# Attention turns: the score maxima from four packed groups of 32 rows, one bank per head, instead of sixteen full-height tiles

## The reference, cut to what matters

```python
x = x + jnp.tanh(g_xattn[0]) * _L0_xattn_ref(_layernorm(x), ctx_1024, ctx_1024, ...)
x = x + jnp.tanh(g_ffn[0])   * _L0_ffn_ref(_layernorm(x), ...)
x = x + jnp.tanh(g_xattn[1]) * _L1_xattn_ref(_layernorm(x), ctx_1024, ctx_1024, mask, ...)
x = x + jnp.tanh(g_ffn[1])   * _L1_ffn_ref(_layernorm(x), ...)
```

```python
scores = jnp.einsum('bhqd,bhkd->bhqk', q, k) / jnp.sqrt(jnp.float32(D_K))
probs = jax.nn.softmax(scores, axis=-1)
out = jnp.einsum('bhqk,bhkd->bhqd', probs, v)
```

## Time and profile before

| | |
|---|---|
| three runs | 1334.78, 1335.67, 1332.43 us |
| median | 1334.78 us |
| the profiled execution: its span, first to last instruction | 1338.1 us |
| instructions | 28180 |
| mean granted TensorE clock, as a share of full speed | 0.984 |

### The profile page before, as it was taken

One profiled execution on the slowest core, in us unless ns is written; L12 is line 12 of the kernel. 1 busy time (PEld: TensorE's weight loads), 2 busy tenths in 40 slices (PEclk: granted clock), 3 DMA queues, 4 the chain that ended last, 5 costly groups with the idle time before them and its releaser, 6 DMA issues.

```text
span 1338.1 us, 28180 instructions
## 1 busy us (share of the span) xinstructions
PE 1256.4 (94%) x10584; PEld 903.2 (67%) x10584; DVE 886.5 (66%) x1568; ACT 570.1 (43%) x1039; POOL 553.4 (41%) x454
## 2 busy tenths in 40 slices
PE   6999999999999968887999999999997999999997
PEld 6777776777777657621446666766675788888886
DVE  5984677777676455564546766766675977777762
ACT  3255345434442554453553443343336434333331
POOL 3312642553251100000329667955734644454440
PEclk9999999999999998999899999999998999999999
DMA  9865455234411677899983643564414111111100
GB/s 334 231 173 185 140 181 172 74 114 148 140 67 41 206 216 247 297 386 363 400 340 122 220 170 103 163 218 135 126 41 159 63 63 63 63 63 41 53 31 32
DMA packets 126262, 213.58 MB, mean 160 GB/s; under 512 B 27497, under 2 KB 49001, under 8 KB 122091
## 3 DMA queue, kind: packets, MB, share of 16 engines
q1 hardware_dynamic: 126187, 212.57, 47.5%
HBM read 129.92 MB, written 82.62 MB: 159 GB/s over the span
## 4 chain that ended last, share of the span: by engine, by line
PE 81%; DVE 5%; DMA 4%; ACT 4%; issue 3%; SPq 2%; POOL 1%; ACTq 0%; DVEq 0%; POOLq 0%
PE b L157 14%; PE b L158 13%; PE b L159 13%; PE b L1573 5%; PE b L1771 5%; PE b L1772 4%; PE b L1773 4%; PE b L1545 4%; PE b L2067 3%; PE b L1678 3%; PE b L2101 2%; PE b L1686 2%; DMA s_rp<-e_chosen 2%; PE b L2085 2%; PE b L1593 2%
## 5 line engine op out<-in xcount | busy, mean ns | idle before, releaser
L1137 ACT ACTIVATE a_pr<-b 120x512 f32<-120x512 f32 x252 | 130.1, 603 | 95.1 <-PE b L1573 95.1
L1326 DVE TENSOR_REDUCE a_mx<-b 128x4 f32<-128x480 f32 x256 | 151.8, 649 | 12.9 <-PE b L1545 12.8
L1019 POOL TENSOR_TENSOR a_rp<-a_rp,a_b2s 128x512 f32<-128x512 f32 x96 | 120.4, 1293 | 24.9 <-DMA a_rp<-s_rp 24.9
L1058 POOL TENSOR_TENSOR a_atl<-a_pvs,a_ath 128x512 fp32r<-128x512 f32 x64 | 81.2, 1300 | 82.4 <-ACT a_ath L1181 82.4
L1771 PE MATMUL b<-a_woh,a_ath 128*128 128x512 f32 x256 | 104.7, 409 | 3.1 <-POOL a_atl L1058 3.1
L157 PE MATMUL b<-a_xth,a_wqh 128*128 128x512 f32 x256 | 104.0, 406 | 0.3 <-DVE a_xtl L1301 0.3
L1772 PE MATMUL b<-a_wol,a_ath 128*128 128x512 f32 x256 | 101.4, 396 | 0.0
L158 PE MATMUL b<-a_xtl,a_wqh 128*128 128x512 f32 x256 | 101.4, 396 | 0.0
L159 PE MATMUL b<-a_xth,a_wql 128*128 128x512 f32 x256 | 101.4, 396 | 0.0
L1773 PE MATMUL b<-a_woh,a_atl 128*128 128x512 f32 x256 | 101.3, 396 | 0.0
L1003 POOL TENSOR_TENSOR a_rstd<-a_ve,a_mhalf 128x4 f32<-128x4 f32 x16 | 16.2, 1013 | 191.9 <-DVE a_ve L1248 191.9
(11 more groups left out here) (237 smaller groups left out, 3130.5 us busy)
## 6 DMA issues: line engine op xcount, KB each, us to landing
a_rp<-s_rp SPq DMA_DIRECT2D x128, 256.0 KB, 4.5
s_x<-a_x SPq DMA_DIRECT2D x16, 1024.0 KB, 4.3
s_rp<-e_chosen SPq DMA_DIRECT2D x16, 1024.0 KB, 7.9
s_rp<-e_xc SPq DMA_DIRECT2D x16, 1024.0 KB, 7.9
e_w<-in_w SPq DMA_DIRECT2D x56, 256.0 KB, 4.8
a_xr<-in_x_t SPq DMA_DIRECT2D x8, 1024.0 KB, 6.3
a_x<-in_x SPq DMA_DIRECT2D x8, 1024.0 KB, 11.0
s_xn<-a_xn SPq DMA_DIRECT2D x8, 1024.0 KB, 4.8
```

The costliest lines, as they stand in the source:

```text
L1019: pool.tensor_tensor(rp[:, t, a], rp[:, t, a], b2s[:, :], ALU.add).then_inc(rp_biased, 1)
L1058: pool.tensor_tensor(quarter(atl, q), quarter(pvs, q), f(quarter(ath, q)), ALU.subtract).then_inc(a_lo, 1)
L1137: act.activation(pr[:, h % RING, :], bank[k][0:S2, :], ACT.Exp, scale=SCALE)\
L1326: dve.tensor_reduce(mx[:, t, :, r], bank[k][:, 0:HJ * S2].rearrange("p (a s) -> p a s", a=HJ), AX.X, ALU.max).then_inc(free[k], 1)
```

## The change

A new function `max_group` makes the maxima of four heads at once for all 512 queries. Head b of the group uses its own 32 rows of the array and its own bank `s{b}`: the stationary operand is the 32x128 part of `qh`, the moving one the 32x120 block of `kbd`, and query tile t fills columns t*120 to (t+1)*120 of the bank. Sixteen matmuls, t outside and b inside, take the place of four; the last four signal the banks. Before them it waits for the query (`q_hi`) and for all four banks. `maxima` reads the same 480 columns of a bank, which are now four query tiles of one head, and writes them at the transposed place of `mx`.

The order on TensorE is now: query 1, wait for the keys, group 0, query 2, (choices), group 1, query 3, group 2, output tile 0, group 3, output tiles 1 to 3. VectorE alternates the low part of query m with the maxima of group m - 1.

```diff
@@ maxima, VectorE @@
-                dve.tensor_reduce(mx[:, t, :, r], bank[k][:, 0:HJ * S2].rearrange("p (a s) -> p a s", a=HJ),
+                dve.tensor_reduce(mx[:, t, :, r] if i is None else mx[:, :, t, r],
+                                  bank[k][:, 0:HJ * S2].rearrange("p (a s) -> p a s", a=HJ),
                                   AX.X, ALU.max).then_inc(free[k], 1)
@@ turn, VectorE @@
-                queries(j, (1, 2))
-                maxima(i, 0)
-                maxima(i, 1, (0, 1))
-                queries(j, (3,))
-                maxima(i, 1, (2, 3))
-                maxima(i, 2)
+                for m in range(1, C):
+                    queries(j, (m,))
+                    maxima(i, m - 1)
@@ TensorE, new @@
+        def max_group(i, j, r):
+
+            pe.wait_ge(q_hi, C * j + r + 1)
+            for b in range(HJ):
+                k, use = max_bank(i, r, b)
+                pe.wait_ge(free[k], use)
+            for t in range(NT):
+                for b in range(HJ):
+                    k, at = max_bank(i, r, b)[0], slice(b * DK, (b + 1) * DK)
+                    ins = pe.matmul(bank[k][:, t * S2:(t + 1) * S2], qh[at, r, t * P:(t + 1) * P],
+                                    kbd[at, r, b * S2:(b + 1) * S2], start=True, stop=True)
+                    if t == NT - 1:
+                        ins.then_inc(full[k], 1)
@@ turn, TensorE @@
                 queries(i, 1)
+                pe.wait_ge(kbd_in, 16 * HJ * (i + 2))
+                max_group(i, i + 1, 0)
                 queries(i, 2)
             if tail and not last_:
                 choices(i)
             if not last_:
-                pe.wait_ge(kbd_in, 16 * HJ * (i + 2))
-                for t in range(NT):
-                    max_tile(i, i + 1, 0, t)
+                max_group(i, i + 1, 1)
                 queries(i, 3)
-                for t in range(NT):
-                    max_tile(i, i + 1, 1, t)
+                max_group(i, i + 1, 2)
@@ output tiles, behind matmuls m of tile t @@
-                        if t < 2:
-                            max_tile(i, i + 1, 2 + t, m)
+                        if t == 0 and m == C - 1:
+                            max_group(i, i + 1, 3)
```

## The result

The changed kernel took 1355.1 us (median of 4 runs, 1351.5 to 1357.9), the kernel before 1335.2 on the same chip. The ratio is 1.0133, with an interval from 1.0112 to 1.0154: **17.7 us slower**, 15.0 to 20.6 by the interval. The two medians alone lie 19.9 us apart; ratios and intervals stand on record beside the medians and differ from theirs by some 2 us, and this document goes by the ratios. The forecast had the direction, but with +9.4 us it had about half of the size, and its range ended at 1352. The profiled execution of the changed kernel took 1352.4 us, with a span of 1350.6.

What follows compares the result with a forecast made beforehand. TensorE, busy 94% of a 1338.1 us span, was taken as the bound. Terms 6.9 + 0.5 - 0.6 + 2.6 gave +9.4 us on 1334.8, so 1344.2; range 1341 to 1348, or 1337 to 1352 reaching into rivals.

Steps and rivals of the forecast that it cites:

- the wait of a group for VectorE: Before groups in both layers: TensorE waits for VectorE to free the banks, 0.10 to 0.30 us, signal estimated at 0.06.
- the stall for the keys: Ahead of group 0 in layer 1, turns 1 to 5: TensorE idles 0.9 to 1.95 us until the keys land.
- Part 1: TensorE's matmuls in the 14 changed turns: a group costs 0.79 us against four tiles' 0.88, saving 5.7 us in all.
- Part 2: VectorE must free all four banks before each group; waits per turn 0.41 us in layer 0, 0.60 in layer 1.
- -0.1 a turn: Layer 0, turns 1 to 6: waits of 0.41 us against 0.5 saved by the matmuls; -0.6 us in all.
- Part 3: Keys wanted 2.80 us sooner: +6.9 us in layer 1, turns 1 to 5; turn 0 of layer 0 also waits.
- landing is issue plus the time shown: Key loads on SP's queue: landing taken as issue time plus time shown, as 846.4 + 4.2 = 850.6 in turn 3.
- +2.6: Turn 0 of layer 0: the second query falls behind the wait for the keys, so the stretch takes 16.1 us against 13.56.
- Rival 3: Clock falls after layer 1 stalls of 1.4 us and more, four or five times, adding +7 to +8.5 us; chance 0.12.
- Rival 1: VectorE and keys are ahead of TensorE everywhere, so matmuls decide: -5.7 us, 1329.1, or 1298 at quarter price; chance 0.06.

Runs made afterwards that it cites:

- e7: The kernel before, with its old tiles, keys issued amid the experts' loads and the spread's multiplications ahead of query 0's low part; 1340.47 us, ratio 1.0035.
- e1: The kernel before with only TensorE's wait for the next keys moved, from behind query 2 to ahead of it; 1347.93 us, ratio 1.0085.

## Why the prediction was right in direction and short in size

The forecast was +9.4 us, 1344.2, with a range to 1352; measured were 17.7 us by the ratio and a median of 1355.1. The three causes that it named, matmuls, VectorE and keys, are all there. The steps that failed are terms of the sum: the wait of a group for VectorE, where 0.06 us was put behind VectorE's end and 0.14 came; the stall for the keys, where nothing was put between landing and matmul and some 0.4 us came, and where each turn's slack was read from one execution; and the low clock in layer 1, which was left out of the sum as a rival with a chance of 0.12, and came to 3.0 us, 1.5 of them behind a stall for the keys.

**Part 1, TensorE's own work: right.** 0.79 us a group was forecast, and 0.78 measured; 0.34 and 0.5 us a turn were to be saved, and 0.30 and 0.46 are, where nothing waits. The Trainium skill (TensorEngine Tiling (Array Packing), "Theoretical Speedup") gives up to 4x, that is down to a quarter of the tiles' 0.88; the row of the group shows 0.78. The same page ("Key Properties") says that a change of the tiling mode drains the engine, and the edges agree: from 280.59 to the group are 0.32 us where a step is 0.233, and from 281.50 to the next matmul 0.34. A step of 0.33 stands also behind a plain wait without a change of form (278.15 to 278.48 in e7), so the second edge is no more than a restart of the stream takes there.

**Part 2, VectorE: right in kind, mis-sized.** The term "-0.1 a turn" in layer 0 came out as +0.2. TensorE and VectorE there:

```profile
281.66 0.66 PE L1546 MATMUL b<-a_kbd,a_qh 32*128 32x120 f32 x16 [0.31 <-DVE a_pvs L1447]
...
293.11 0.66 PE L1546 MATMUL b<-a_kbd,a_qh 32*128 32x120 f32 x16 [0.21 <-DVE a_mx L1326]
```
```profile
279.04 2.48 DVE L1447 TENSOR_TENSOR a_pvs<-b,a_pvs 128x512 f32<-128x512 f32 x4
...
290.63 2.34 DVE L1326 TENSOR_REDUCE a_mx<-b 128x4 f32<-128x480 f32 x4
```

The multiplications end at 281.52 and the group starts at 281.66; the maxima end at 292.97 and the group starts at 293.11. From VectorE's end to TensorE's start are **0.14 us** both times, and 0.14 to 0.15 ahead of every group that VectorE held in any execution. The forecast had estimated 0.06, between 0.03 and 0.04 of other pairs and 0.08 of a landing. It is no constant of this pair of engines: in e7 VectorE's low part ends at 277.41 + 0.68 = 278.09 and the query tile starts at 278.15, 0.06 later, and the spread of the kernel before, a packed form as well, shows 0.06 in turn 3 of layer 1:

```profile
844.37 1.28 DVE L1432 SCALAR_TENSOR_TENSOR a_rx<-a_rx,a_part,a_rs 128x128 fp32r<-128x128 f32 x1
```
```profile
845.71 0.67 PE L1698 MATMUL b<-a_rx,a_bc 32*128 32x128 f32 x16 [0.26 <-DVE a_rx L1432]
```

In turn 0 of that layer it was 0.15 (709.12 to 709.27). What makes it long ahead of the groups stays open. Against the stretches without a wait, the two waits delay the turn by 0.37 and 0.28 us, where 0.27 and 0.14 were forecast. With the 0.04 less that the matmuls save this is the 0.3 us a turn, 2.0 us in all.

In turns 0 and 6 of layer 1 another step failed too: VectorE's schedule was read in turn 3 and taken for all. VectorE in turn 6, of the kernel before and then of the changed one:

```profile
983.53 0.75 DVE L1316 SCALAR_TENSOR_TENSOR a_ql<-b,a_bq,a_qh 128x512 fp32r<-128x512 f32 x1 [1.70 <-ACT a_qh L1093]
984.20 2.47 DVE L1446 TENSOR_TENSOR a_pvs<-b,a_pvs 128x512 f32<-128x512 f32 x4
```
```profile
996.68 0.75 DVE L1316 SCALAR_TENSOR_TENSOR a_ql<-b,a_bq,a_qh 128x512 fp32r<-128x512 f32 x1 [1.69 <-ACT a_qh L1093]
997.35 2.48 DVE L1447 TENSOR_TENSOR a_pvs<-b,a_pvs 128x512 f32<-128x512 f32 x4
```

Before, the multiplications of this turn end at 984.20 + 2.47 = 986.67, 3.37 us after the query's start at 983.30; in turn 3 it was 3.04, as the low part there was early. So group 0 waits 0.45 us in turn 6 instead of the forecast's 0.10. The answer stood in the trace of before, one turn further on. Together the two turns cost 1.1 us without the clock, 0.6 more than forecast.

**Part 3, the keys: right in kind, the largest term, and short by 2.4 us.** TensorE in the changed kernel, turn 0 of layer 0, then turn 3 of layer 1:

```profile
144.41 0.98 PE L1546 MATMUL b<-a_kbd,a_qh 32*128 32x120 f32 x16 [4.58 <-DMA a_kbd<-s_kh]
...
857.56 0.66 PE L1546 MATMUL b<-a_kbd,a_qh 32*128 32x120 f32 x16 [1.49 <-DMA a_kbd<-s_kh]
```

and the last two key loads of turn 3 on SP's queue, with their time to landing:

```profile
L680 SPq DMA_DIRECT2D a_kbd<-s_kh x2: 316/316/317, 852.4 to 852.8; - x2
DMA to landing us min/median/max: 3.7/4.0/4.3
```

852.8 + 4.3 = 857.1, and the group starts at 857.56. The step that failed is "landing is issue plus the time shown", with nothing behind it: from landing to the matmul are some 0.4 us here, where turn 0 of layer 0 had shown 0.08. Neither the group nor the layer alone makes it: in e1, where a query tile waits for the same keys in layer 1, it is 0.10 to 0.19 us, ahead of the groups there 0.35 to 0.5, and ahead of the groups in turn 0 of layer 0 up to 0.1. The stalls were forecast as 1.95, 1.4, 1.4, 0.9 and 1.4 us, and came as 1.95, 1.26, 1.49, 1.74 and 1.97. Turns 4 and 5 are furthest off, and that is the second half of it: each turn was priced by its own slack in one execution. Before, TensorE waited 0.59 and 0.22 us for the reciprocals ahead of the spread in these turns, which gave the keys time; in the changed kernel it didn't wait there. The way of the keys is nearly the same everywhere: from SP's load of the permutation to group 0 are 857.56 - 838.91 = 18.65 us in turn 3, 18.44 and 18.53 in turns 4 and 5, and 18.66 and 17.96 in turns 1 and 2. The sixteen loads' 11.43 us, the keys and their flight make a chain of nearly fixed length, and this chain, not TensorE, now sets where group 0 starts. Of the 2.4 us, 1.8 are these stalls (8.4 us of idle time for 7.05, and 0.08 more each: idle time counts from the end of the matmul before, 0.40 us behind its start, where a group without a wait comes 0.32 behind it), 0.5 is the wait ahead of group 2 (0.40 us a turn for 0.30) and 0.2 the matmuls' smaller saving.

In turn 0 of layer 0 +1.7 us came for +2.6, since the keys let group 0 start 0.75 us sooner after the spread than the tiles had started in the execution of before. Over six other executions with all the group's columns there, the stretch took 25.01 to 26.62 us, +1.1 to +2.7: this term goes by when the loads land. With tiles it goes by that too: 21.60 us in e7, where the keys were waited for 1.02 us and no clock fell, for 23.95.

**Rival 3, the clock, came in part.** It was priced at four or five falls in layer 1. In turn 4:

```profile
904.95 0.66 PE L1546 MATMUL b<-a_kbd,a_qh 32*128 32x120 f32 x16 [1.74 <-DMA a_kbd<-s_kh]
905.54 0.62 PE L157 MATMUL b<-a_xth,a_wqh 128*128 128x512 f32 x1
905.96 0.63 PE L158 MATMUL b<-a_xtl,a_wqh 128*128 128x512 f32 x1
```
```profile
904.95:909.00 4.05, 4.05 (x25) 3.20 (x26) 2.35 (x4) 0.02 (x1) 4.05 (x4) 0.60 0.71 234
```

Steps of 0.42 us instead of 0.233, and the next group comes 5.13 us after this one instead of 3.59: 1.5 us lost. The stalls of 1.95 and 1.97 us in turns 1 and 5 had no such sequel. In turn 0 the clock was low for a like time behind the wait for the reciprocals (1.78 us), which stands in the kernel before as well (1.89 us, with no low clock behind); those 1.5 us are in the stretches' sum, but nothing shows that the change caused them. Over the twelve executions the clock fell there in four, all with groups, and not in the eight others, the three with tiles among them, though that wait was 1.5 to 2.3 us in all.

In sum, of the 7.1 us that the forecast lacked, 2.4 lie in the keys of layer 1, 2.0 in VectorE's waits of layer 0, 0.6 in those of layer 1, and 3.0 in the clock, less 0.9 in turn 0 of layer 0. By the experiments' ratios, the keys in layer 1 cost about 8.4 us with the clock behind their stalls, VectorE's waits about 10 (11.6 by the ratio) in a kernel whose keys come in time, turn 0 of layer 0 about 3.3 (1.9 in the stretch), and without all three the kernel is 5.6 us faster than before; each of these differences is uncertain by some 3 us. By the stretches the matmuls save 6 x 0.46 + 7 x 0.30 = 4.9 us, a little less than the 5.7 forecast. Rival 1 (TensorE decides) did not come, but it is what the kernel does once keys and VectorE have been moved out of its way.

## What to carry to other kernels

When work moves ahead on an engine's stream, list every input it takes with it and follow each back to the queue that issues it: here a transfer behind sixteen others on one queue made up about half of the loss, and some 8 us came back with one edit to the order of the issues. Replacing four separate buffers by all four at once takes away the slack that let a slower engine trail, so every 0.1 us in that engine's chain then counts: moving its order took back about 10 us. Read the schedule in every turn instead of in one. A restructuring that loses can still be the right one: judge it again when its inputs come in time, and against the old form with the same edits.

## What the runs showed of the hardware

- From VectorE's end to TensorE's start were 0.14 to 0.15 us ahead of the groups and 0.05 to 0.06 ahead of a query tile (e7); ahead of the spread both came. From the landing of the last keys to TensorE were 0 to 0.1 us in turn 0 of layer 0, and in layer 1 0.10 to 0.19 ahead of a query tile (e1) and 0.35 to 0.5 ahead of the groups. What makes the differences stays open.
- A packed group of sixteen matmuls took 0.59 us with 120 moving columns and 0.56 with 60.
- Of the waits for the keys in layer 1, over all profiled executions, the matmuls behind the wait ran at 1.2 GHz in 9 of the 18 cases with 1.6 us or more, and in none of the 10 with less. One fall cost about 1.5 us, and the costliest, after 2.47 us, 2.9; the fall after the longest wait, 2.78 us, cost 1.5. Which of the longer stalls is followed by a fall could not be told from the traces.
